# Graph stage of a four-layer network kernel: the routed tokens' chain one step later, the first sum ahead of the statistics, warming products moved

## The reference, cut to what matters

```python
x = x + _L1_gnn_ref(_layernorm(x, axis=-1), w_rel1, w_root1, b1, w_rel2, w_root2, b2, adj, adj)
x = x + _L1_ffn_ref(_layernorm(x, axis=-1), Wr, W1s, b1s, W2s, b2s, W1p, b1p, W2p, b2p)

def conv(x, w_rel, w_root, b):            # per relation: masks = (adj == 1)
    out = jnp.einsum('bnd,de->bne', x, w_root) + b
    agg = jnp.einsum('bij,bid->bjd', masks[r], x) / deg[r]
    return out + jnp.einsum('bjd,de->bje', agg, w_rel[r])
h = jax.nn.elu(conv(encoded_spans, w_rel1, w_root1, b1))
h = jax.nn.elu(conv(h, w_rel2, w_root2, b2))

shared = gelu(x @ W1s + b1s) @ W2s + b2s
rw = jax.nn.softmax(x @ Wr, axis=-1)      # 8 experts
topw, topi = jax.lax.top_k(rw, 2)
```

## Time and profile before

| | |
|---|---|
| Time, median of 3 | 2728.17 us (2725.9 to 2731.24) |
| The profiled execution | 2732.5 us, of it the span of the instructions 2730.6 us |
| Busy in the span | PE 97%, weight loads 78%, DVE 71%, POOL 55%, ACT 54% |
| Granted TensorE clock, mean of the span | 0.984 |
| Graph steps, 1556 to 1998 us | about 442 us for 32 steps |
| Shared feed-forward work behind them, to 2073 us | about 75 us |
| Expert stage, from 2075 us | to the end |

### The profile page before, as it was taken

One profiled execution on the slowest core, in us unless ns is written; L12 is line 12 of the kernel. 1 busy time (PEld: TensorE's weight loads), 2 busy tenths in 40 slices (PEclk: granted clock), 3 DMA queues, 4 the chain that ended last, 5 costly groups with the idle time before them and its releaser, 6 DMA issues. The chain is left out here.

```text
span 2730.6 us, 85746 instructions
## 1 busy us (share of the span) xinstructions
PE 2636.5 (97%) x28783; PEld 2141.0 (78%) x28784; DVE 1928.5 (71%) x6630; ACT 1471.2 (54%) x2930; POOL 1499.3 (55%) x2542
## 2 busy tenths in 40 slices
PE   8999999899989999999999899899998999999999
PEld 4666666589968888888888677777788999999888
DVE  5777777567779999999999588777864544555453
ACT  2555555455547777777767455444553444444444
POOL 5555555333335555555555367676752666666664
PEclk8999999999999999999999999999999999999999
DMA  1111111000000000000000011111511222222264
GB/s 53 32 35 35 35 31 44 10 0 0 0 2 1 0 0 0 0 0 0 0 0 1 25 53 59 55 52 56 161 64 46 77 77 77 77 77 77 81 200 139
DMA packets 158118, 118.26 MB, mean 43 GB/s; under 512 B 20151, under 2 KB 145594, under 8 KB 158011
## 3 DMA queue, kind: packets, MB, share of 16 engines
q1 hardware_dynamic: 140602, 81.02, 10.7%
q0 software_dynamic: 17408, 35.95, 3.9%
HBM read 68.36 MB, written 48.56 MB: 43 GB/s over the span
## 5 line engine op out<-in xcount | busy, mean ns | idle before, releaser
L2027 POOL DMA_INDIRECT token_y<-e_y,e_rows x288 | 295.7, 1027 | 78.8 <-issue 76.6
L2070 ACT ACTIVATE e_hidden<-e_ps,e_b1g 128x512 f32<-128x512 f32 x288 | 194.6, 688 | 258.8 <-PE e_ps L90 258.1
L1303 POOL DMA_INDIRECT sorted_z<-r_z,r_rows x256 | 264.3, 1032 | 67.1 <-issue 63.9
L2122 PE MATMUL e_ps<-expert_w,e_hidden 128*128 x2304 | 280.3, 275 | 0.0
L2122 PEld LDWEIGHTS e_ps<-expert_w,e_hidden 128*128 128x128 f32 x2304 | 273.9, 192 | 6.3
L514 DVE TENSOR_REDUCE a_V<-a_ps_s 128x8 f32<-128x1024 f32 x128 | 156.9, 1226 | 131.0 <-PE a_ps_s L394 131.0
L842 POOL TENSOR_TENSOR s_share<-s_att,s_rsum 128x256 f32<-128x256 f32 x128 | 78.7, 615 | 309.5 <-DVE s_rsum L1117 309.5
L2199 DVE TENSOR_TENSOR e_biased<-e_ps,expert_b 128x512 f32<-128x512 f32 x72 | 49.8, 692 | 213.8 <-PE e_ps L2122 213.8
L394 PE MATMUL a_ps_s<-a_nT 16*128 16x128 f32 x2048 | 186.0, 300 | 0.1
L402 PE MATMUL a_ps_st<-a_topT,a_nT 17*128 17x128 f32 x2048 | 184.7, 298 | 0.1
L394 PEld LDWEIGHTS a_ps_s<-a_nT 16*128 16x128 f32 x2048 | 136.5, 188 | 45.8 <-issue 45.5
(11 more groups left out here) (400 smaller groups left out, 8123.8 us busy)
## 6 DMA issues: line engine op xcount, KB each, us to landing
e_z<-sorted_z SPq DMA_DIRECT2D x72, 260.0 KB
c_y<-token_y SPq DMA_DIRECT2D x22, 512.0 KB, 4.2
X<-in_x_dram SPq DMA_DIRECT2D x32, 256.0 KB, 2.8
a_adj<-in_adj_dram SPq DMA_DIRECT2D x32, 256.0 KB, 2.8
g_adj<-in_adj_dram SPq DMA_DIRECT2D x32, 256.0 KB, 2.9
out_dram<-X SPq DMA_DIRECT2D x32, 256.0 KB, 2.5
c_y_s<-token_y SPq DMA_DIRECT2D x10, 512.0 KB, 4.9
token_y<-e_y,e_rows POOLq DMA_INDIRECT x288
```

Of the source, the lines that this page charges most:

```text
L1303: nc.gpsimd.indirect_dma_start(sh.sorted_z, bass.IndirectOffsetOnAxis(ap=rows[own][:, e * GB + piece:e * GB + piece + 1], axis=0), zr[own] ...
L2027: nc.gpsimd.indirect_dma_start(sh.token_y, bass.IndirectOffsetOnAxis(ap=rows[p][:, b:b + 1], axis=0), y[p][:, b, :], None).then_inc(y_scat ...
L2070: nc.scalar.activation(hidden[p][:, c, :], ps_1[c % 2][:, :], ACT.Gelu, bias=b1g[p][:, c:c + 1]).then_inc(s["hidden_done"], 1)
L2122: last = nc.tensor.matmul(ps_2[q][:, b, :], hidden[q][:, f, b * T:(b + 1) * T], w2[:, bass.ds(e, 1), f * D:(f + 1) * D].squeeze(1), start= ...
```

## The change

Everything that a routed group needs behind its normalization moves by one step, and three things are reordered within a step:

1. The turn of `r_z`, its copy to `r_zT` and the logits and two largest now handle group t - 2 instead of t - 1; ranks, rows and gates handle t - 3 instead of t - 2; the scatters handle t - 3 and t - 4. `LAG` is 4. The statistics, the normalization of `r_z` and the twin stay at t - 1.
2. On DVE the first sum stands ahead of the statistics; ranks into rows (`r_place_of`, `r_rows_f`) stand ahead of `g_h`; the normalization of `r_z` stands behind `g_h` and the gates.
3. On PE the turn of `r_z` stands between the turn of `z` and the degrees, with 4 warming products ahead and 5 behind it (9 and 1 before); the 15 warming products of step 31 are gone; the shared work of the last steps is spread over one more step, with other counts in POOL's pauses.

The core of the diff:

```diff
-        LAG, PEEL = 3, 8
+        LAG, PEEL = 4, 8
@@ GpSimd
-                if live(known, 2, groups):
+                if live(known, 3, groups):
-                    pool.wait_ge(s["rows_done"], t - 1)
+                    pool.wait_ge(s["rows_done"], t - 2)
-                        pool.wait_ge(f["up_done"], (9, 21)[known - groups])
+                        pool.wait_ge(f["up_done"], (5, 13, 21)[known - groups])
-                    scatter((k + 2) % 4, 0)
+                    scatter((k + 1) % 4, 0)
@@ TensorE
                     turned(z[q])
-                    keep_warm(9)
-                    pe.wait_ge(s["edge_done"], t + 2)
-                    ...
-                    degrees(q)
-                if known == groups:
-                    shared(2)
-                    shared(3)
-                if live(known, 1, groups):
-                    keep_warm(1 if live(known, -1, groups) else 15 if live(known, 0, groups) else 0)
-                    pe.wait_ge(s["zr_done"], t)
+                    keep_warm(4)
+                if live(known, 2, groups):
+                    pe.wait_ge(s["zr_done"], t - 1)
...
                     last.then_inc(s["zr_turned"], 1)
+                if live(known, -1, groups):
+                    keep_warm(5)
+                    pe.wait_ge(s["edge_done"], t + 2)
+                    pe.wait_ge(s["degree_done"], t + 1)
+                    if since(known, 3):
+                        pe.wait_ge(s["place_done"], t - 2)
+                        pe.wait_ge(s["carried"], t - 2)
+                    degrees(q)
+                if known == groups:
+                    shared(2)
+                if known == groups + 1:
+                    shared(4)
@@ ScalarE
-                if live(known, 1, groups):
-                    act.wait_ge(s["zr_turned"], t)
+                if live(known, 2, groups):
+                    act.wait_ge(s["zr_turned"], t - 1)
@@ VectorE
+                if live(known, 0, groups):
+                    dve.wait_ge(s["gathered1"], t + 1)
+                    dve.wait_ge(s["root1_copied"], t + 1)
+                    dve.wait_ge(s["rdeg_done"], t + 1)
+                    summed(sum1, ps_g1, k, s["sum1_done"])
                 if live(known, 1, groups):
                     dve.wait_ge(s["x_done"], t)
```

More of the change, by code:

```diff
@@ L1505, in step @@
                     last.then_inc(s["h_turned"], 1)
[L1506 to L1509 removed]
+                if live(known, 2, groups):
+                    pe.wait_ge(s["zrT_done"], t - 1)
                     pe.wait_ge(s["degree_done"], t + 2 if known is None else min(known + 2, groups))
[L1511 to L1513 removed]
+                    if since(known, 3):
+                        pe.wait_ge(s["place_done"], t - 2)
+                        pe.wait_ge(s["carried"], t - 2)
                     for b in range(GB):
@@ L1537, in step @@
                 if known == groups:
+                    shared(3)
+                if known == groups + 1:
                     shared(5)
@@ L1578, in step @@
                     nc.scalar.activation(neg2[:, :, :], neg2[:, :, :], ACT.Exp, scale=-1.0).then_inc(s["exp2_done"], 1)
-                if live(known, 2, groups):
-                    act.wait_ge(s["gap_done"], t - 1)
-                    if since(known, 3):
-                        act.wait_ge(s["gates_set"], t - 2)
+                if live(known, 3, groups):
+                    act.wait_ge(s["gap_done"], t - 2)
+                    if since(known, 4):
+                        act.wait_ge(s["gates_set"], t - 3)
                     nc.scalar.activation(odds[:, 0, :], gap[:, :], ACT.Exp).then_inc(s["odds_done"], 1)
-                if known == groups:
-                    shared(2)
-                    shared(3)
                 if live(known, 0, groups):
@@ L1606, in step @@
                     nc.scalar.activation(neg1[:, :, :], neg1[:, :, :], ACT.Exp, scale=-1.0).then_inc(s["exp1_done"], 1)
-                if live(known, 1, groups):
-                    act.wait_ge(s["zr_turned"], t)
-                    if since(known, 2):
-                        act.wait_ge(s["logits_done"], t - 1)
+                if live(known, 2, groups):
+                    act.wait_ge(s["zr_turned"], t - 1)
+                    if since(known, 3):
+                        act.wait_ge(s["logits_done"], t - 2)
                     nc.scalar.activation(zrT[:, :], ps_z[:, :], ACT.Copy).then_inc(s["zrT_done"], 1)
+                if known == groups:
+                    shared(2)
+                    shared(3)
                 if live(known, 0, groups):
@@ L1763, in step @@
+                if live(known, 3, groups):
+                    dve.wait_ge(s["ranked"], t - 2)
+                    if since(known, 4):
+                        dve.wait_ge(s["carried"], t - 3)
                     nc.vector.tensor_tensor(place[:, :, :], ps_r[:, 1, :, :],
-                                            carry[p][:, :].unsqueeze(1).to_broadcast([T, GB, EXPERTS]),
+                                            carry[q][:, :].unsqueeze(1).to_broadcast([T, GB, EXPERTS]),
                                             ALU.add).then_inc(s["place_done"], 1)
-                    nc.vector.tensor_tensor(carry[q][:, :], carry[p][:, :], ps_r[:, 2, 0, :],
+                    nc.vector.tensor_tensor(carry[p][:, :], carry[q][:, :], ps_r[:, 2, 0, :],
@@ L1767, in step @@
                                             ALU.add).then_inc(s["carried"], 1)
-                if known == groups:
-                    f_low(1)
-                    f_norm(2)
-                if live(known, 1, groups):
-                    dve.wait_ge(s["rstd_done"], t)
-                    if since(known, 5):
-                        dve.wait_ge(scattered[(k + 3) % 4], (r - 1 + (k + 3) // 4) * 2 * GB * 16)
-                    nc.vector.tensor_copy(sh.mean[:, bass.ds((t - 1) * GB, GB)], meanvar[q][:, :, 0])
-                    normalized(zr[(k + 3) % 4][:, :, 0, :], t - 1, meanvar[q], sh.rstd, s["zr_done"])
+                    dve.wait_ge(s["place_done"], t - 2)
@@ L1810, in step @@
                     inverse_degrees((k + 1) % 4)
+                if known == groups:
+                    f_low(1)
+                    f_norm(2)
+                if live(known, 1, groups):
+                    dve.wait_ge(s["rstd_done"], t)
+                    if since(known, 5):
+                        dve.wait_ge(scattered[(k + 3) % 4], (r - 1 + (k + 3) // 4) * 2 * GB * 16)
+                    nc.vector.tensor_copy(sh.mean[:, bass.ds((t - 1) * GB, GB)], meanvar[q][:, :, 0])
+                    normalized(zr[(k + 3) % 4][:, :, 0, :], t - 1, meanvar[q], sh.rstd, s["zr_done"])
                 if known == groups - 1:
                     f_split()
-                if known == groups:
-                    f_low(2)
-                    f_norm(3)
-                    f_add(0)
+                if known == groups + 1:
                     f_low(3)
@@ L1848, in step @@
                 if known == groups:
+                    f_low(2)
+                    f_norm(3)
+                    f_add(0)
+                if known == groups + 1:
                     f_low(4)
```

107 lines of the change are left out of this document (44 added, 63 removed).

## The result

The changed kernel takes **2682.24 us** (median; 2681.56 to 2690.77) against 2728.41 us of the kernel before beside it on the same chip (2725.9 to 2731.24): a ratio of 0.984, 95% interval 0.982 to 0.986. The forecast was 2704 (2695 to 2719). The profiled execution has a span of 2679.8 us, before 2730.6.

The account below looks back on a forecast made before the run. Bound: a ring of waits through four engines, 13.94 us a step, to become 12.53, taken as 12.75. Front 4.9, loop 18.1, three steps 2.2, end -1: 24.2 us gained, median 2728.17 to 2704 (8 in 10: 2695 to 2719).

Parts of the forecast that it names:

- The ring: Chain of waits from one second sum to the next through the engines, `g_h` included: 12.53 us a step, before 13.94.
- The shade of 0.2 us on it: Allowance for small slips from bounds close to the ring: 12.75 us a step taken, range 12.53 to 13.1.
- three near bounds: DVE's work of 12.1 us a step, POOL's of 12.35, and ACT's twin, ending at 10.5 ahead of a copy wanted at 10.53.
- Jumps: The loop's four jumps back: 3.6 us each before, 4.4 after, with 0.3 for less DVE slack and 0.5 for a slow gather.
- the ring is all there is: Rival: 12.53 us a step and jumps at 3.6 as before, 35 us gained, 2693 us; under 2697, chance 0.07.
- POOL or the twin: Rival: POOL's scatters or ACT's twin copy become the bound, 13.1 us a step, 2714.5 us; 2709 to 2720, chance 0.23.
- PE ahead of `g_h`'s turn: PE's work ahead of that turn, the degrees last, is ready at 7.8 for 7.99 us: hidden, with 0.2 us of cover.
- PE cold in every step: Rival: a longer idle stretch puts PE at 1.2 GHz each step, 1.8 us a step lost, 2758 us; chance 0.06.
- The end: One step more, ACT table changes and PE perhaps at 1.2 GHz in step 31: 1 us lost, bounds 0 to 3.

Follow-up runs that it names:

- n = 29, 64: The changed kernel with 29 or 64 tiny memsets at the head of DVE's graph block, which move its loop's start: 2694.66 us (29) and 2696.27 us (64).
- e9: The changed kernel with `place_of` and its sum behind `g_h` instead of ahead of it: 2688.24 us.
- e7: The changed kernel without the nine warming products around the turn of `r_z`: 2743.12 us.
- e15: The changed kernel with 122 tiny memsets at the head of DVE's graph block: 2684.76 us.
- e10: The changed kernel with 200 tiny memsets at the head of DVE's graph block: 2706.24 us.
- e3: The changed kernel with the first sum put back behind the statistics, all else as changed: 2714.16 us.
- e12: e9 with ACT's twin copy behind its copy of `g_y` instead of ahead of it: 2681.59 us.
- e17: e12 with 4+4 warming products around the turn of `r_z` instead of 4+5: 2684.22 us.
- e16: e12 with 4+2 warming products around the turn of `r_z` instead of 4+5: 2712.92 us.

## Why the forecast was right and wrong, step by step

- **The ring**: right. 12.53 us computed, 12.52 measured; `g_h` at 7.25 for 7.26, the wait of the first sum 0.38 for 0.2.
- **The shade of 0.2 us on it** ("small slips will show: I take 12.75"): wrong for most of it. The three near bounds were counted rightly and hid behind the ring in most steps instead of adding to it; the mean step of the loop is 12.58. Front 2.4, loop 3.4 and the three steps 1.3 us: 7.1 of the 26.6 us that the spans gained beyond the forecast. Of the 1.3, 0.6 is no shade: one of the three steps before took 14.13 where the sum has 13.49.
- **Jumps** ("DVE's 3.09 us start when it is done ... 3.6 + 0.3 + 0.5 = 4.4 us a jump"): the step that failed, 17.6 us. I took the stall as a property of the jump and asked only how it would be covered. It is a property of where the loop stands, and the change moved the loop by 28 instructions. The packets were in the profile of the kernel before; I did not ask what the "issue" was. Where the loop of the changed kernel does stand badly (n = 29, 64), the jump costs 3.6 us and the kernel takes 2695 to 2696, the lower end of the range. The rival "the ring is all there is", 2693 with jumps of 3.6, describes those two runs within 2 and 4 us. With jumps that cost nothing and all else as forecast, the sum would have been 41.8 us.
- **POOL or the twin**: did not bind in three steps of four, and cost 0.2 us in the fourth. POOL's waits fell to 0.2 a step. In five of the loop's steps its power took 1.52 us, DVE waited 0.2 for it, and the twin held up the copy of `g_y`: steps of 12.70, 1 us in all. The rival had priced 13.1 for every step. The twin bound in every step when 0.42 us of DVE's work was put ahead of it (e9). The Trainium skill (SBUF — State Buffer, Who interferes with whom) gives VectorE and GpSimd a shared pair of ports under an exclusive lock. That would fit here: in the loop the long power starts 0.07 us behind the start of DVE's `g_h`, and the short one 0.06 ahead of it. No run tests it. Single scatters differ too, 0.95 to 1.47 us.
- **PE ahead of `g_h`'s turn** ("hidden, with 0.2 us of cover"): hidden, but with no cover left. The weight loads of the degrees end 7.99 us behind the start of the second sum, where the forecast had 7.8, those of the turn begin at 7.98 without a wait (7.99 forecast), and DVE's clip waits 0.18 for the degrees.
- **PE cold in every step** (2758): did not come, and the price was about right: e7, at a clock of 0.85, has it, 2.0 us a step for 1.8.
- **The end** (-1, 0 to 3 of loss): the last step lost 0.5 with PE at a clock of 0.69 to 0.74. That loss is not steady: in e15, the same code but for the memsets, the clock is 1.00 and then 0.72 there, and the step takes 15.34 as before. What follows it was 1 us shorter: the kernel before has a clock of 0.66 from 2000 to 2010, the changed one 1.00 from 1950 on. Net gain 0.5 to 1 where a loss of 1 was forecast.
- Sum: 24.2 forecast, 50.8 on the spans. Jumps 17.6, the shade 7.1, the end 2.

## What to carry to other kernels

An idle time marked "issue" at the first instruction of a loop's round is a question about instruction fetch: compare the packets of the instruction queue in the loop's later rounds with those of its first. Any edit that changes how many instructions stand ahead of a loop can add or remove such stalls, here 13.5 us for five instructions, so before a small gain or loss is credited to an edit, see whether the packets changed too. And a move that makes something later is safe only once nothing on the ring waits for what it delays: the same move of the first sum gained 32 us or lost 101, depending on where the rest stood.

## What the chip showed that was not expected

- DVE's loop of 347 instructions is fetched anew, in 5 packets of 8 KB a round, at starts 115, 22, 30 and 66 modulo 128, and not at 80, 87 or 110 (one of 346: yes at 115, no at 90). The stall is 3.0 to 3.2 us, the price in the step 3.6.
- DVE halts 0.34 and 0.33 us at the borders of two pieces, 128 short instructions apart (e10).
- In e3 PE idles 0.51 to 0.65 us ahead of `g_h`'s turn in every step, and in ten of them the product two operations later ran at the low clock (2.07 for 1.16 us), while the changed kernel, which has no idle time there, stays at 1.00. In e12's order nine products (of 0.21 to 0.25 us) go with a clock of 1.00, eight (e17) with 0.99 and one slow step, six (e16) with 0.91 and two slow steps of three.
